# A 12-layer attention stack on one core: the scores of a tile issued as one block, and the value products cut to 64 rows by 64 columns

## The chip, the core and the metric

The kernel runs on one core of a Trainium2 chip. The time is device microseconds of one execution, lower is better; several runs are made and the median counts. TensorE (PE in the profile, with its weight loads shown apart as PEld), VectorE (DVE), ScalarE (ACT), GpSimd (POOL) and SyncE (SP, which issues the DMAs) each run a queue of their own in order, and wait for each other on semaphores.

## What is computed

The input is 2048 tokens of 128 channels. A stack of six layers runs on it, then a state space block (the "mamba" part), then the same six layers again. Half of each stack's output is added to its input. Each layer is attention in windows of 32 tokens, then a gated feed-forward part of 341 hidden units. Of the attention this is what matters here:

```python
def local_attention(q, k, v):            # 16 heads of 64, windows of w = 32
    nw = n // w
    bk2, bv2 = (look(bk), look(bv))      # a window and the one before it: 64 keys
    sim = jnp.einsum('bhwie,bhwje->bhwij', bq, bk2) * QK_SCALE
    sim = jnp.where(mask, -jnp.finfo(sim.dtype).max, sim)
    attn = jax.nn.softmax(sim, -1)
    out = jnp.einsum('bhwij,bhwje->bhwie', attn, bv2)
    return out.reshape(b, h, n, d)
...
out = local_attention(q, k, v).transpose(0, 2, 1, 3).reshape(b, n, INNER)
return out @ Wo
```

## The kernel before

**Tiles and steps.** The tokens are cut into 16 tiles of 128 (four windows each), so that a stack has 6 x 16 = 96 tiles and both stacks have 192. A tile passes through some six software-pipelined steps: at step s TensorE works on the k projection of tile s-19, the q projection of tile s-18, the value products of tile s-22 and so on. The loop over `s` in `tensor_stack` (L694 to L714) writes the order out by hand, and the other engines have loops of the same kind. Nothing else decides the order. Every fourth tile closes a chunk of 512 tokens, for which the feed-forward part runs. So four steps in a row differ: two are plain; one also has the centring product (L451) and the variance product (L471) of a chunk, one on each side of the P transposes, and its up products (L492 to L494) follow two blocks after the value products; one has the carry product (L341) and the down products (L550) between the scores and the P transposes. They are called the variance step and the down step below.

**PSUM.** It is used as four slots of two banks. Slot 0 takes the q and the k projection in turn. Slot 2 takes, in turn, the v projection, P transposed, and q transposed. Slot 3 takes the scores and the result of the value products. Slot 1 takes k transposed and small results. A block of TensorE waits until the last user's result has been read out.

**Scores.** For each of 8 head pairs, 4 windows and 2 heads of the pair one product is made: 32 queries by 64 channels against 64 channels by 64 keys (L349). It uses 64 rows and 32 columns of the array, so the array is cut in 8 parts that are used in turn; the two heads of a pair write to different banks. Eight mask products (L359) go ahead. The 64 products stand in two blocks: `scores_low` has head pairs 0 to 3, near the end of a step, and `scores_high` has 4 to 7, first in the next step. Between them stand the P transposes (L282) of the tile before. A float32 product is recorded as two pairs of weight load and matmul, so each half is "x64" in the trace.

**P and the value products.** `exponentials` (ScalarE, L996) writes P, GpSimd scales it by the reciprocal sums (L1774), and `p_transpose` turns it with 8 transposes, each with two heads' 64 keys stacked on 128 partitions. `p_evacuate` (L1010) copies the result from slot 2 to PTS, one activation for the upper 64 partitions and one for the lower. They go to different columns of PTS, which is 2048 wide and was set to zero at first (L1788 and, for the second stack, L1803). Each block of 64 columns is so block diagonal, and one product of 128 rows by 64 columns against 64 columns of PTS makes a window's output for both heads (`value_products`, L408): 32 of them for a tile, "x64" in the trace. `o_evacuate` (L1019) copies the result to OTS, and `out_products` (L428) multiplies by Wo. The values stand in V2, which ten small DMAs on SyncE's queue fill for each tile (`spread_values`).

**The chain of the rotation.** After the q projection ScalarE squares it (L921), and VectorE makes the two halves of the rotation from PSUM (L1304, L1313). Then slot 0 is free, and only then may the k projection begin. For k these are L934, L1322 and L1331, after which comes the next q projection. VectorE's order in a step is L1304, L1313, L1345 (sums of squares), [L1471 and L1473 after a down product], L1363 (row maximum of the scores), [L1403 and L1405 in a variance step], L1371 (scores minus maximum), L1322, L1389 and L1390 (residual), L1331, L1351, L1378 (row sums of P), L1382, L1357. The value products wait for L1371 of the next tile, since they write over its scores in slot 3.

Of the kernel before, what the change touches and what calls it, by code (L numbers as in the profile page):

```python
# [9 lines left out]
ACT = mybir.ActivationFunctionType  # L10
# [6 lines left out]
N = NT * NL  # L17
# [14 lines left out]
def build(nc, xT, consts, wqkv, wo, w1, w2, lpar, qks, mpar, in_w, xp_w, dt_w, out_w, out):  # L32
    ctx = ExitStack()
    with ctx:
# [3 lines left out]
        def sem(name):  # L38
            return ctx.enter_context(nc.semaphore("s_" + name))
# [23 lines left out]
        PS = ctx.enter_context(nc.psum_tensor("PS", [128, 4, 1024], F32))  # L63
        PSB = PS[:, :, :].rearrange("p s (h n) -> p (s h) n", h=2)
        top = [0]

        def take(n):
            top[0] += n
            assert top[0] <= 34400, top[0]
            return ARENA[:, top[0] - n:top[0]]  # L70

        def heads(ap, n=H):
            return ap.rearrange("p (h d) -> p h d", h=n)
# [19 lines left out]
        T2 = take(1024)  # L93
        KT = [take(1280) for _ in range(2)]
        SB, P, OTS = (take(1024) for _ in range(3))
        PTS = take(2048)
        V2 = [take(2048) for _ in range(2)]
        HG = take(1536)
        SX, RS, XC = HG[:, 0:512], HG[:, 512:1024], HG[:, 1024:1536]
# [34 lines left out]
        def unit(u):  # L134
# [10 lines left out]
        wo_in = [sem(f"wo_in{i}") for i in range(2)]  # L145
        w1_in, inw_in, mw_in = sem("w1_in"), sem("inw_in"), sem("mw_in")
        v2_in = [sem(f"v2_in{i}") for i in range(2)]
        eps_set, pad_set, zero_set, masks_set, edge_set, tab_set = (sem(n) for n in (
            "eps_set", "pad_set", "zero_set", "masks_set", "edge_set", "tab_set"))
        i_mu, i_sq, i_var, i_ln, i_rs, i_done = (sem("i_" + n) for n in (  # L150
            "mu", "sq", "var", "ln", "rs", "done"))
        x_hi, x_lo, w1_hi, w1_lo = (sem(n) for n in ("x_hi", "x_lo", "w1_hi", "w1_lo"))
# [7 lines left out]
        qT_ev, kT_ev, PT_ev, oT_ev = (sem(n + "_ev") for n in ("qT", "kT", "PT", "oT"))  # L160
# [37 lines left out]
        def tensor_stack(pe, r):  # L198
# [162 lines left out]
                            MK[a:b, 64:128].unsqueeze(1).broadcast_to([64, 8, 64]), start=True, stop=False,  # L361
                            skip_group_check=True)

            def scores_low(n):
                if not 0 <= n < N:
                    return
                pe.wait_ge(qT_ev, n0 + n + 1)
                pe.wait_ge(kT_ev, n0 + n + 1)
                pe.wait_ge(car_ev, n0 + n + 1)
                if n == 0:  # L370
                    pe.wait_ge(i_done, 4 * r + 4)
                    if r == 0:
                        pe.wait_ge(masks_set, 1)
                s = n + 20
                if (s - 24) % 4 == 3:
                    after_chunk(pe, f_h[1], (s - 24) // 4)
                after_tile(pe, oT_ev, s - 22)
                if s < RAMP or s >= N:
                    after_chunk(pe, f_h[1], (s - 23) // 4 - 1)
                    after_tile(pe, sub_done, s - 21)  # L380
                score_masks(n)
                score_tiles(n, range(4))

            def scores_high(n):
                if 0 <= n < N:
                    score_tiles(n, range(4, 8)).then_inc(S_done, 1)

            def p_transpose(n):
                if not 0 <= n < N:
# [8 lines left out]
                transposes(2, P, PT_done)  # L398

            def value_products(n):  # L400
                pt = PTS.rearrange("p (h w x) -> p h w x", h=8, w=4)
                v2 = V2[n % 2].rearrange("p (w h d) -> p w h d", w=4, h=8)
                for m in range(4):
                    for win in range(4):
                        for side in range(2):
                            hp, col = 2 * m + side, 32 * win
                            out = PS[64 * side:64 * side + 64, 3, 256 * m:256 * m + 256]
                            last = nc.tensor.matmul(  # L408
                                out.rearrange("p (a q) -> p a q", a=2)[:, :, col:col + 32], v2[:, win, hp, :],
                                pt[:, hp, win, :], start=True, stop=True, skip_group_check=True)  # L410
                last.then_inc(pv_done, 1)

            def values(n):
# [11 lines left out]
            def out_products(n, bank):  # L425
                w = WO[n // NT % 2]
                for j in range(8):
                    last = nc.tensor.matmul(PSB[:, bank, 0:128], w[:, 128 * j:128 * j + 128], OTS[:, 128 * j:128 * j + 128],  # L428
                                            start=j == 0, stop=j == 7)
                last.then_inc(wo_done, 1)  # L430

# [142 lines left out]
            def finish_tiles():  # L574
# [4 lines left out]
                    pe.wait_ge(sem, c0 + u + 1)  # L579

                u = UNITS - 3
                scores_high(94)
                tile(k_nrm, 95)
                tile(k_rot, 95)
                transposes(0, KN[1], kT_done)
# [108 lines left out]
            for s in range(115):  # L694
                if s == 19 + 1:
                    var_in(pe, r, 3)
                scores_high(s - 21)
                k_project(s - 19)
                out_project(s - 23)
                q_transpose(s - 20)  # L700
                values(s - 22)
                k_transpose(s - 20)
                ffn_up0(s - 24)
                ffn_up1(s - 24)
                ffn_up2(s - 24)
                q_project(s - 18)
                v_project(s - 20)
                scores_low(s - 20)
                carry(s - 19)
                ffn_centre(s - 23)  # L710
                ffn_down(s - 24)
                p_transpose(s - 21)
                ffn_variance(s - 23)
# [140 lines left out]
        def scalar_stack(act, r):  # L854
# [144 lines left out]
            def p_evacuate(n, slot=2):  # L999
                if not 0 <= n < N:  # L1000
                    return
                act.wait_ge(PT_done, n0 + n + 1)
                if n >= 1:
                    act.wait_ge(pv_done, n0 + n)
                else:
                    act.wait_ge(zero_set, r + 1)
                blocks = PTS.rearrange("p (b a q) -> p b a q", a=2, q=32)
                for par in range(2):
                    a, b = 64 * par, 64 * par + 64
                    last = act.activation(blocks[a:b, :, par, :], PS[a:b, slot, :].rearrange("p (b q) -> p b q", q=32), ACT.Copy)  # L1010
                last.then_inc(PT_ev, 1)

            def o_evacuate(n):
                if not 0 <= n < N:
# [698 lines left out]
        def pool_stack(pool, r):  # L1713
# [71 lines left out]
            if r == 0:  # L1785
                nc.gpsimd.memset(VT[1], 0.0)
                nc.gpsimd.memset(KT[1], 0.0).then_inc(pad_set, 1)
                nc.gpsimd.memset(PTS, 0.0).then_inc(zero_set, 1)  # L1788
            low_weights(0, 0)
            low_input(0)  # L1790
            low_weights(0, 1)
# [5 lines left out]
            for s in range(113):  # L1797
                if s == 17 + 1:
                    low_weights(0, 2)
                    low_input(1)  # L1800
                if s == 17 + 3 and r == 1:
                    pool.wait_ge(m_out, 4)
                    nc.gpsimd.memset(PTS, 0.0).then_inc(zero_set, 1)  # L1803
                if s == 17 + 5:
                    low_input(2)
                if s == 17 + 8:
                    low_input(3)
                ffn_low(s - 23)
                k_add_halves(s - 18)
                p_normalise(s - 20)  # L1810
                w_low_k(s - 18)
                q_normalise(s - 18)
                q_add_halves(s - 17)
                k_normalise(s - 18)
                input_low(s - 24)
                w_low_v(s - 19)
                w_low_q(s - 17)
# [259 lines left out]
```

## Time and profile before

| | |
|---|---|
| median of 3 runs | 3331.24 us (3329.32 to 3331.4) |
| span of the profiled execution | 3329.5 us |
| PE busy, and its weight loads | 3179.2 us (95%), 2524.1 us (76%) |
| DVE, ACT, POOL busy | 2793.2 us (84%), 2503.3 us (75%), 2435.9 us (73%) |
| TensorE share of the chain that ended last | 79% |
| value products L408, busy | 403.7 us |
| scores L349, busy | 326.0 us |
| copies of P transposed L1010, busy | 390.5 us |

A row of the timeline gives the start and the length of a merged run of instructions. A matmul is pipelined, and its recorded length holds some 0.2 us in which the next ones already run. So the time that a block takes on the engine is read from its start to the start of the next block, and not from its busy time. The "idle before" of a row is counted from the modelled end of the instruction before.

### The profile page before, as it was taken

How to read it: one execution, taken by the hardware profiler on the slowest of the kernel's cores; microseconds unless marked ns; L12 is line 12 of the kernel's file. 1: busy time of each engine (PE TensorE's matmuls, PEld its weight loads, DVE VectorE, ACT ScalarE, POOL GpSimd, SP SyncE). 2: the span in 40 equal slices, each digit the busy share in tenths (PEclk: the TensorE clock that was granted, in tenths of full speed). 3: DMA queues.
4: the chain of work that ended last, by engine and by line, in shares of the span. 5: the costliest groups of instructions: out<-in, count | busy, mean ns of one | idle time of the engine just before them, and what ended most of it. 6: DMA issues, size and time to landing. Idle time of an engine off the chain costs nothing.

```text
span 3329.5 us, 120453 instructions
## 1 busy us (share of the span) xinstructions
PE 3179.2 (95%) x51630; PEld 2524.1 (76%) x51630; DVE 2793.2 (84%) x3207; ACT 2503.3 (75%) x3160; POOL 2435.9 (73%) x1229
## 2 busy tenths in 40 slices
PE   7999999999999999998888999999999999999999
PEld 5888888888887887875333778788788888788777
DVE  7888888888888888877999888888888888888886
ACT  5777777777777777777676777777777777778776
POOL 6777777777777776672999768768768768768664
PEclk8999999999999999999999999999999999999999
DMA  3333333233233232221000323323323323323222
GB/s 120 84 75 87 74 82 89 71 86 88 67 90 85 67 90 65 65 72 38 30 0 0 97 67 81 86 69 86 89 70 82 95 67 80 96 65 85 69 65 69
DMA packets 142299, 245.22 MB, mean 74 GB/s; under 512 B 32397, under 2 KB 34638, under 8 KB 141774
## 3 DMA queue, kind: packets, MB, share of 16 engines
q1 hardware_dynamic: 141774, 237.51, 28.0%
q8 instruction: 415, 6.80, 0.9%
q14 instruction: 110, 0.90, 0.1%
HBM read 35.01 MB, written 1.05 MB: 11 GB/s over the span
## 4 chain that ended last, share of the span: by engine, by line
PE 79%; DVE 7%; issue 7%; POOL 4%; ACT 3%; DMA 0%; SPq 0%; DVEq 0%; POOLq 0%; ACTq 0%
PE PS L282 15%; PE PS L408 11%; PE PS L428 8%; PE PS L214 8%; PE PS L216 7%; PE PS L215 7%; PE PS L349 6%; PE PS L550 4%; ACT ARENA L955 3%; PE PS L492 2%; PE PS L494 2%; PE PS L493 2%; POOL ARENA L1868 2%; PE PS L451 2%; DVE ARENA L1681 2%
## 5 line engine op out<-in xcount | busy, mean ns | idle before, releaser
L1760 POOL TENSOR_TENSOR ARENA<-ARENA,RN 128x1024 f32<-128x1024 f32 x192 | 365.6, 1904 | 456.0 <-ACT RN L945 456.0
L282 PE MATMUL PS<-C,ARENA 128*128 128x128 f32 x4608 | 615.0, 277 | 42.9 <-ACT ARENA L955 16.4
L1752 POOL TENSOR_TENSOR ARENA<-ARENA 128x1024 f32<-128x1024 f32 x192 | 468.3, 2439 | 228.9 <-DVE ARENA L1331 228.1
L282 PEld LDWEIGHTS PS<-C,ARENA 128*128 128x128 f32 x4608 | 512.9, 141 | 119.7 <-issue 76.4
L214 PE MATMUL PS<-WL,XH 128*128 128x512 f32 x1152 | 489.7, 425 | 7.3 <-POOL XL L1719 4.0
L1010 ACT ACTIVATE ARENA<-PS 64x1024 f32<-64x1024 f32 x384 | 390.5, 1017 | 98.0 <-PE PS L282 94.6
L1746 POOL TENSOR_TENSOR ARENA<-ARENA 128x1024 f32<-128x1024 f32 x192 | 457.3, 2382 | 7.0 <-DVE ARENA L1313 7.0
L216 PE MATMUL PS<-WH,XH 128*128 128x512 f32 x1152 | 454.2, 394 | 0.0
L215 PE MATMUL PS<-WH,XL 128*128 128x512 f32 x1152 | 452.1, 392 | 0.0
L408 PE MATMUL PS<-ARENA 128*64 128x64 f32 x12288 | 403.7, 224 | 42.0 <-DVE ARENA L1371 26.0
L408 PEld LDWEIGHTS PS<-ARENA 128*64 128x64 f32 x12288 | 378.7, 139 | 77.1 <-issue 77.1
L1304 DVE TENSOR_TENSOR ARENA<-PS,TAB 128x1024 f32<-128x1024 f32 x192 | 235.0, 1224 | 230.5 <-ACT ARENA L921 230.5
L1774 POOL TENSOR_TENSOR ARENA<-ARENA,RI 128x1024 f32<-128x1024 f32 x192 | 365.9, 1906 | 47.2 <-DVE RI L1382 37.3
L428 PEld LDWEIGHTS PS<-ARENA 128*128 128x128 f32 x3072 | 372.2, 191 | 17.8 <-ACT ARENA L1019 1.5
L1768 POOL TENSOR_TENSOR ARENA<-ARENA,RN 128x1024 f32<-128x1024 f32 x192 | 374.2, 1949 | 1.5 <-ACT RN L945 1.5
L428 PE MATMUL PS<-ARENA 128*128 128x128 f32 x3072 | 373.7, 275 | 1.1 <-ACT ARENA L1019 1.1
L349 PEld LDWEIGHTS PS<-ARENA 64*32 64x32 f32 x24576 | 292.4, 105 | 69.3 <-issue 59.0
L349 PE MATMUL PS<-ARENA 64*32 64x64 f32 x24576 | 326.0, 223 | 0.1
L1363 DVE TENSOR_REDUCE MX<-PS 128x16 f32<-128x1024 f32 x192 | 234.2, 1220 | 94.8 <-PE PS L349 92.9
L1019 ACT ACTIVATE ARENA<-PS 128x1024 f32<-128x1024 f32 x192 | 197.1, 1027 | 139.0 <-PE PS L408 139.0
L921 ACT ACTIVATE ARENA<-PS 128x1024 f32<-128x1024 f32 x192 | 197.2, 1027 | 93.6 <-PE PS L216 93.6
L214 PEld LDWEIGHTS PS<-WL,XH 128*128 128x128 f32 x1152 | 218.3, 189 | 62.4 <-POOL XL L1719 4.8
(160 smaller groups left out, 6476.1 us busy)
## 6 DMA issues: line engine op xcount, KB each, us to landing
ARENA<-ARENA SPq DMA_DIRECT2D x1152, 128.0 KB
ARENA<-ARENA SPq DMA_DIRECT2D x768, 64.0 KB
ARENA<-in_wqkv SPq DMA_DIRECT2D x36, 512.0 KB, 5.1
ARENA<-in_wo SPq DMA_DIRECT2D x12, 512.0 KB, 3.9
ARENA<-in_w SPq DMA_DIRECT2D x12, 341.0 KB, 3.5
ARENA<-in_w SPq DMA_DIRECT2D x12, 192.0 KB, 3.9
X<-in_xT SPq DMA_DIRECT2D x4, 256.0 KB, 6.0
out<-X SPq DMA_DIRECT2D x1, 768.0 KB, 3.6
```

The costliest lines, as they stand in the source:

```text
L214: nc.tensor.matmul(o, XH[:, x], WL[:, s], start=True, stop=False)
L215: nc.tensor.matmul(o, XL[:, x], WH[:, s], start=False, stop=False)
L216: last = nc.tensor.matmul(o, XH[:, x], WH[:, s], start=False, stop=True)
L282: last = nc.tensor.transpose(PS[:, slot, 128 * j:128 * j + 128], src[:, 128 * j:128 * j + 128], ident)
L349: last = nc.tensor.matmul(PS[32 * win:32 * win + 32, slot, c:c + 64], q[a:b, hp, 32 * win:32 * win + 32], kt[a:b, hp, 32 * win:32 * win + ...
L408: last = nc.tensor.matmul(out.rearrange("p (a q) -> p a q", a=2)[:, :, col:col + 32], v2[:, win, hp, :], pt[:, hp, win, :], start=True, st ...
L428: last = nc.tensor.matmul(PSB[:, bank, 0:128], w[:, 128 * j:128 * j + 128], OTS[:, 128 * j:128 * j + 128], start=j == 0, stop=j == 7)
L1010: last = act.activation(blocks[a:b, :, par, :], PS[a:b, slot, :].rearrange("p (b q) -> p b q", q=32), ACT.Copy)
L1746: nc.gpsimd.tensor_tensor(QN[n % 2], QN[n % 2], P if n == 1 else T2, ALU.add).then_inc(q_add, 1)
L1752: nc.gpsimd.tensor_tensor(KN[n % 2], KN[n % 2], T2, ALU.add).then_inc(k_add, 1)
L1768: nc.gpsimd.tensor_tensor(a, a, bc(RN[:, n % 2, 16:32], 64), ALU.mult).then_inc(k_nrm, 1)
L1774: nc.gpsimd.tensor_tensor(heads(P), heads(P), bc(RI[:, n % 2, :], 64), ALU.mult).then_inc(p_nrm, 1)
```

## The change

The two score blocks become one, `scores`, where `scores_low` stood; the P transposes of the tile before then follow all 64 score products. P transposed is copied from PSUM by one activation over 128 partitions, to a PTS that is 1024 wide and has no zeros; both memsets of PTS are gone, and the first copy of the second stack waits for `m_out` itself. 1024 columns behind it are left unused. The value products are 64 instead of 32: each takes one head alone, 64 rows (its keys) by 64 columns (its channels) against 32 columns (its queries). The two heads of a pair use the upper and the lower 64 rows and write to different banks; two pairs use the left and the right 64 columns. OTS then holds the heads in another order, and `out_products` takes the blocks of Wo in that order.

```diff
-        PTS = take(2048)
+        PTS = take(1024)
+        take(1024)
...
-            def scores_low(n):
+            def scores(n):
...
                 score_masks(n)
-                score_tiles(n, range(4))
-
-            def scores_high(n):
-                if 0 <= n < N:
-                    score_tiles(n, range(4, 8)).then_inc(S_done, 1)
+                score_tiles(n, range(8)).then_inc(S_done, 1)
...
-                pt = PTS.rearrange("p (h w x) -> p h w x", h=8, w=4)
+                pt = heads(PTS, 8)
...
                     for win in range(4):
-                        for side in range(2):
-                            hp, col = 2 * m + side, 32 * win
-                            out = PS[64 * side:64 * side + 64, 3, 256 * m:256 * m + 256]
-                            last = nc.tensor.matmul(
-                                out.rearrange("p (a q) -> p a q", a=2)[:, :, col:col + 32], v2[:, win, hp, :],
-                                pt[:, hp, win, :], start=True, stop=True, skip_group_check=True)
+                        for par in range(2):
+                            for side in range(2):
+                                hp, a, b, col = 2 * m + side, 64 * par, 64 * par + 64, 32 * win
+                                o = 512 * par + 128 * m + col
+                                last = nc.tensor.matmul(
+                                    PS[64 * side:64 * side + 64, 3, o:o + 32], v2[a:b, win, hp, :],
+                                    pt[a:b, hp, col:col + 32], start=True, stop=True, skip_group_check=True)
...
+                    i = 2 * (j % 4) + j // 4
+                    last = nc.tensor.matmul(PSB[:, bank, 0:128], w[:, 128 * i:128 * i + 128], OTS[:, 128 * j:128 * j + 128],
...
-                scores_high(s - 21)
                 k_project(s - 19)
...
-                scores_low(s - 20)
+                scores(s - 20)
...
                 else:
-                    act.wait_ge(zero_set, r + 1)
-                blocks = PTS.rearrange("p (b a q) -> p b a q", a=2, q=32)
-                for par in range(2):
-                    a, b = 64 * par, 64 * par + 64
-                    last = act.activation(blocks[a:b, :, par, :], PS[a:b, slot, :].rearrange("p (b q) -> p b q", q=32), ACT.Copy)
-                last.then_inc(PT_ev, 1)
+                    act.wait_ge(m_out, 4 * r)
+                act.activation(PTS, PS[:, slot, :], ACT.Copy).then_inc(PT_ev, 1)
...
-                nc.gpsimd.memset(PTS, 0.0).then_inc(zero_set, 1)
...
-                if s == 17 + 3 and r == 1:
-                    pool.wait_ge(m_out, 4)
-                    nc.gpsimd.memset(PTS, 0.0).then_inc(zero_set, 1)
```

On TensorE, in a variance step, before (L359 masks, L349 scores, L451 centring product, L282 transposes of P, L471 variance product, L214 first product of the k projection):

```order
L359 MATMUL PS<-MK 32x512 x8
L349 MATMUL PS<-ARENA 32x64 x32
L451 MATMUL PS<-ARENA,C 128x512
L282 MATMUL PS<-C,ARENA 128x128 x8
L471 MATMUL PS<-ARENA,C 128x512
L349 MATMUL PS<-ARENA 32x64 x32
L214 MATMUL PS<-WL,XH 128x512
```

The same place after (the numbers of the lines are one higher or lower from here on: L350 scores, L450, L283 and L470 as L451, L282 and L471 before):

```order
L360 MATMUL PS<-MK 32x512 x8
L350 MATMUL PS<-ARENA 32x64 x64
L450 MATMUL PS<-ARENA,C 128x512
L283 MATMUL PS<-C,ARENA 128x128 x8
L470 MATMUL PS<-ARENA,C 128x512
L215 MATMUL PS<-WL,XH 128x512
```

The second block of 32 score products has moved ahead of the centring product, and the k projection now follows the variance product. In a plain step L451 and L471 are absent from both lists, and the transposes stood between the two score blocks.

On TensorE, later in a step, from the out products to the k transposes, before (L428 out products, L282 transposes of q and then of k, L408 value products):

```order
L428 MATMUL PS<-ARENA 128x128 x8
L282 MATMUL PS<-C,ARENA 128x128 x8
L408 MATMUL PS<-ARENA 64x2x32 x32
L282 MATMUL PS<-C,ARENA 128x128 x8
L492 MATMUL PS<-XNH,W1L 128x512
```

After:

```order
L427 MATMUL PS<-ARENA 128x128 x8
L283 MATMUL PS<-C,ARENA 128x128 x8
L406 MATMUL PS<-ARENA 64x32 x64
L283 MATMUL PS<-C,ARENA 128x128 x8
L491 MATMUL PS<-XNH,W1L 128x512
```

Nothing has moved here; 32 products over 64 columns (2 x 32) have become 64 over 32.

## Rows read from the trace of the kernel before

**Rows 1.** The page, its first part: busy us (share) x instructions.
```profile
PE 3179.2 (95%) x51630; PEld 2524.1 (76%) x51630; DVE 2793.2 (84%) x3207; ACT 2503.3 (75%) x3160; POOL 2435.9 (73%) x1229
```

**Rows 2.** Who waited for whom: engine line <- line: us in total, times, longest.
```profile
PE PS L408 <- DVE ARENA L1371: 26.0, 46, 1.3
...
PE PS L282 <- ACT ARENA L955: 16.4, 84, 0.2
```

**Rows 3.** A plain step, timeline, TensorE: start, length, line, [idle before].
```profile
1037.98 0.41 PE L359 MATMUL PS<-MK 64*32 64x512 bf16 x8
...
1038.21 0.84 PE L349 MATMUL PS<-ARENA 64*32 64x64 f32 x64
...
1039.26 1.06 PE L282 MATMUL PS<-C,ARENA 128*128 128x128 f32 x8 [0.21 <-ACT ARENA L955]
...
1040.25 0.86 PE L349 MATMUL PS<-ARENA 64*32 64x64 f32 x64
...
1041.04 0.50 PE L214 MATMUL PS<-WL,XH 128*128 128x512 f32 x1
...
1045.29 2.08 PE L408 MATMUL PS<-ARENA 128*64 128x64 f32 x64
...
1047.30 1.09 PE L282 MATMUL PS<-C,ARENA 128*128 128x128 f32 x8
...
1048.15 0.47 PE L214 MATMUL PS<-WL,XH 128*128 128x512 f32 x1
```

**Rows 4.** The scores of the first tile, timeline, TensorE: the same columns.
```profile
45.61 1.46 PE L349 MATMUL PS<-ARENA 64*32 64x64 f32 x128
47.78 0.47 PE L214 MATMUL PS<-WL,XH 128*128 128x512 f32 x1 [0.71 <-DVE ARENA L1313]
```

**Rows 5.** The same plain step, timeline, VectorE.
```profile
1038.91 1.21 DVE L1313 TENSOR_TENSOR ARENA<-PS,TAB 128x1024 f32<-128x1024 f32 x1
...
1045.55 1.22 DVE L1331 TENSOR_TENSOR ARENA<-PS,TAB 128x1024 f32<-128x1024 f32 x1
```

**Rows 6.** The rotation ahead of the second row of rows 4, VectorE.
```profile
46.31 1.21 DVE L1313 TENSOR_TENSOR ARENA<-PS,TAB 128x1024 f32<-128x1024 f32 x1
```

**Rows 7.** A down step, timeline, TensorE.
```profile
1009.20 0.84 PE L349 MATMUL PS<-ARENA 64*32 64x64 f32 x64
1009.97 0.70 PE L341 MATMUL PS<-ARENA,C 128*128 128x256 f32 x2
...
1013.09 1.04 PE L282 MATMUL PS<-C,ARENA 128*128 128x128 f32 x8
...
1014.84 0.50 PE L214 MATMUL PS<-WL,XH 128*128 128x512 f32 x1
```

**Rows 8.** A variance step, timeline, TensorE.
```profile
1051.31 0.84 PE L349 MATMUL PS<-ARENA 64*32 64x64 f32 x64
1052.09 1.12 PE L451 MATMUL PS<-ARENA,C 128*128 128x512 f32 x2
...
1055.75 0.50 PE L214 MATMUL PS<-WL,XH 128*128 128x512 f32 x1
```

**Rows 9.** The end of that variance step: TensorE's value products, and VectorE.
```profile
1060.51 2.08 PE L408 MATMUL PS<-ARENA 128*64 128x64 f32 x64 [0.45 <-DVE ARENA L1371]
...
1059.15 1.21 DVE L1371 TENSOR_TENSOR ARENA<-PS,MX 128x1024 f32<-128x1024 f32 x1
```

**Rows 10.** Durations in ns, min/median/max: L408 in one step, L349 and L428 everywhere.
```profile
L408 PE MATMUL PS<-ARENA x64: 222/222/270, 1019.1 to 1020.9; 128*64 128x64 f32 x64
...
L349 PE MATMUL PS<-ARENA x24576: 212/216/241, 45.6 to 3293.0; 64*32 64x64 f32 x200
...
L428 PE MATMUL PS<-ARENA x3072: 270/275/377, 76.2 to 3315.1; 128*128 128x128 f32 x192
```

**Rows 11.** What is under way on TensorE at 1027.38, in a score block begun at 1027.14.
```profile
1027.14 0.45 PE L349 MATMUL PS<-ARENA 64*32 64x64 f32 x31
```

**Rows 12.** The second stack's memset of PTS, timeline, GpSimd.
```profile
1841.61 1.80 POOL L1803 MEMSET ARENA<- 128x2048 f32 x1
```

More of the change, by code:

```diff
@@ L147, in build @@
         v2_in = [sem(f"v2_in{i}") for i in range(2)]
-        eps_set, pad_set, zero_set, masks_set, edge_set, tab_set = (sem(n) for n in (
-            "eps_set", "pad_set", "zero_set", "masks_set", "edge_set", "tab_set"))
+        eps_set, pad_set, masks_set, edge_set, tab_set = (sem(n) for n in (
+            "eps_set", "pad_set", "masks_set", "edge_set", "tab_set"))
         i_mu, i_sq, i_var, i_ln, i_rs, i_done = (sem("i_" + n) for n in (
@@ L427, in out_products @@
                 for j in range(8):
-                    last = nc.tensor.matmul(PSB[:, bank, 0:128], w[:, 128 * j:128 * j + 128], OTS[:, 128 * j:128 * j + 128],
+                    i = 2 * (j % 4) + j // 4
+                    last = nc.tensor.matmul(PSB[:, bank, 0:128], w[:, 128 * i:128 * i + 128], OTS[:, 128 * j:128 * j + 128],
                                             start=j == 0, stop=j == 7)
@@ L581, in finish_tiles @@
                 u = UNITS - 3
-                scores_high(94)
                 tile(k_nrm, 95)
```

## The prediction

> **What bounds the kernel now.** I began with the busy shares: PE 95%, the next engine 84% [rows 1]. A busy share of pipelined matmuls proves little, so the next view is who waited for whom. The waits of TensorE are short: in the stacks the largest two are 26 us in 46 places for VectorE's L1371, and 16.4 us in 84 places for ScalarE's L955 [rows 2]. All else is TensorE going from one block to the next. So a change is worth what it takes from TensorE's own sequence, until another chain becomes the later one. The third view is therefore the timeline of each kind of step, read from a block's start to the next block's start.
>
> **One score block, plain step.** Before, from the masks (1037.98) to the k projection (1041.04) there are 3.06 us [rows 3]. In it the first 64 scores take 1.05 to the start of the transposes; in the down step the same block takes 0.77 to its successor (1009.20 to 1009.97) [rows 7]. The 0.28 between is the wait for L955, which reads the v projection out of slot 2 before the transposes may write there.
>
> The new sequence is made of pieces that the trace shows. Masks to scores is 0.23 [rows 3]. The first tile already has all scores in one block, since no transposes are due there: recorded length 1.46 [rows 4], against 0.84 for half. A half gives its place to the successor 0.07 before its recorded end (0.84 against 0.77), so the whole takes 1.39. Transposes with a projection behind them take 0.85 (1047.30 to 1048.15), while those with scores behind them take 0.99 (1039.26 to 1040.25) [rows 3]. Sum: 0.23 + 1.39 + 0.85 = 2.47, and the transposes now come 0.23 + 1.39 = 1.62 after the masks instead of 1.28, so the wait for L955 is gone. The gain is 3.06 - 2.47 = 0.59, of which 0.28 is the wait and 0.31 the switches between kinds of block.
>
> What is late next? The k projection needs slot 0, so it waits for L1313, which ends at 1038.91 + 1.21 = 1040.12 [rows 5]. Where TensorE is known to have waited for it, it began 0.26 after its end (47.78 against 46.31 + 1.21 = 47.52) [rows 4, 6]. That is 1040.38 here; TensorE would arrive at 1037.98 + 2.47 = 1040.45. The gain just fits, with 0.07 to spare; this chain starts at the q projection, ahead of everything that the change touches.
>
> **Down step.** From L349 to the k projection 5.64 (1009.20 to 1014.84), with 3.12 for L341 and L550 (1009.97 to 1013.09) [rows 7]. After: 1.39 + 3.12 + 0.85 = 5.36, so 0.28 less.
>
> **Variance step.** From 1051.31 to 1055.75 there are 4.44 [rows 8]. The first block's 0.77 becomes 1.39, the second (0.79, as 1040.25 to 1041.04 [rows 3]) goes, and some 0.1 of switching with it: about 0.27 less. But the value products of this step already wait for L1371, 0.45 us of idle time, and start at 1060.51 where L1371 ends at 60.36 [rows 9]. Ahead of L1371 VectorE has L1403, which needs the chain from the variance product, and that product is issued 0.6 later than before. So I count 0.06 here.
>
> **Sum of the scores.** The 192 tiles are 48 groups of four steps: 2 x 0.59 + 0.28 + 0.06 = 1.52 us, times 48 = 73 us. The bounds are the switches alone, without any recovered wait (2 x 0.31 + 0.28 = 0.9, so 43 us), and with the variance step at its full 0.27 (83 us). The score semaphore comes earlier too, which nobody on the path waits for: VectorE takes the maximum in its own order behind L1345.
>
> **Value products.** Nothing in this trace runs 64 by 64 parts, so I work out the pace from both sides. The 64 matmuls have a length of 2.08 us together [rows 3], one of them 0.22 [rows 10], so they start (2.08 - 0.22) / 63 = 29.5 ns apart, and with two parts of the array in turn a part has one every 59 ns. The product is not longer than the load: 64 columns more add 275 - 222 = 53 ns. The load of 64 columns, seen bare on the first two products, costs 270 - 222 = 48 ns [rows 10]. So load and product of a part overlap, and a load that starts as the product before it starts sets the pace of 59 ns by itself, with some ns for the handing over. The change halves what is streamed (27 ns) but not the load's 64 columns. With four parts at once, 128 / 4 x 59 ns = 1.89 us; today 64 / 2 x 59 ns = 1.89 us. I take no change. The lower bound is the pace at which score products come, (1.46 - 0.22) / 127 = 9.8 ns [rows 4], so 1.25 us for 128: 0.6 less. The upper bound is a load and a product in turn, 59 + 27 = 86 ns, so 2.75 us: 0.86 more. Zero lies where it does because the score block, which is cut by rows as well, does overlap: its load of 32 columns costs 241 - 216 = 25 ns and its product 53 [rows 10]; in turn that is 78 ns for eight parts, 9.8 each, and only some 24 could have begun 0.24 us into a block, where the trace has 31 [rows 11].
>
> There is a rule against this change. The Trainium skill, TensorE: Matmul & The Clock Gate (Part 3, The mechanism), says that a weight load runs under products in flight only where the row group differs. Left and right parts share their rows, so by it the block before would take 64 x (48 + 53) ns = 6.5 us; it takes 2.01 (1045.29 to 1047.30 [rows 3]), so this trace contradicts it. By the rule the new block would have 64 x (48 + 27) ns = 4.8 us in each half, and the kernel would end some 530 us later; the sum above doesn't use it.
>
> **The copy and the zeros.** ScalarE saves a copy of 1.02 us a tile. It was hidden: the q transposes that need slot 2 come two blocks later, and ScalarE then waits for the k projection anyway. In the drain of each stack the copies stand nearer to the path; I count 1 us there for both. GpSimd's memset in the second stack (1.80 [rows 12]) stands ahead of a k addition while the pipeline fills: 0 to 1.8 us, I take 1. PTS without zeros and the order of Wo cost nothing.
>
> **The sum.** 73 + 1 + 1 = 75 us from the span of 3329.5. The median of the runs is 1.7 above that span, so 3331.2 - 75 = 3256.
>
> **Rivals.**
>
> *The waits come back.* TensorE meets the rotation with 0.07 to spare. If the k projection waits for L1313 by what it saved, a plain step keeps 0.31: 3256 + 48 x 2 x 0.28 = 3283. For it: the small margin. Against: the chain has fixed lengths in every plain step.
>
> *Faster value products.* If the pace is that of issue, 0.6 less a tile. Of that a plain step can use: the q projection, moved to 1048.15 - 0.59 = 1047.56, may start no earlier than 45.55 + 1.22 + 0.26 = 47.03 [rows 5], so 0.53. Four steps give about 2.1, times 48 = 101 us: 3155. The overlap at 59 ns with a load of the same size speaks against it. The Trainium skill, TensorEngine Tiling (Array Packing), Theoretical Speedup, promises up to twice the speed per dimension of at most 64, which would be this case.
>
> *Slower value products, and a slower kernel.* Load and product of a part take turns when the array is cut both ways at 64: 0.86 more a tile, all on the path, 165 us: 3421. It outweighs the scores from 75 / 192 = 0.39 us a tile on, which is a part's round of 71 ns instead of 59. Against it stand the 31 products of rows 11, though those are parts of 32 columns.
>
> **How the numbers follow.** Forecast 68%, with its own range 3235 to 3280 (bounds of the scores, plus a few ns a round). Waits come back 10%, faster products 10%, slower ones 12%. Forecast and first rival together give 78%; 3215 to 3290 holds them and a partial gain in the products. A measurement of this kernel tells about 0.2% from no change. Faster by more than that 87%, within it 2%, slower 11%.
>
> **What would show it.** Right: score blocks of 128 of 1.4 to 1.5 us in all tiles; the wait of the P transposes for L955 gone; masks to k projection near 2.47 in plain steps; value products 2.0 us from start to start. Wrong: that block at 1.3 or 2.7; a wait of the k projection for the rotation of more than 0.1; a variance step that has grown.

## The result, and the profile after

The changed kernel takes 3429.93 us in the median of 4 runs (3428.65 to 3438.7), the kernel before 3330.93 (4 runs). The ratio is 1.030, with an interval of 1.0287 to 1.0316: 99 us slower, where 75 us faster was forecast. The profiled execution of after has a span of 3427.4 us.

**What was changed works as planned.** A plain step of after, timeline, TensorE (start, length, line, count; L360 masks, L350 scores, L283 transposes, L215 first product of a projection, L406 value products; L1364 on VectorE is the subtraction that was L1371):

```profile
1056.09 0.41 PE L360 MATMUL PS<-MK 64*32 64x512 bf16 x8
1056.32 1.46 PE L350 MATMUL PS<-ARENA 64*32 64x64 f32 x128
1057.71 1.09 PE L283 MATMUL PS<-C,ARENA 128*128 128x128 f32 x8
1058.56 0.47 PE L215 MATMUL PS<-WL,XH 128*128 128x512 f32 x1
...
1062.77 2.07 PE L406 MATMUL PS<-ARENA 64*64 64x32 f32 x128
1064.77 1.09 PE L283 MATMUL PS<-C,ARENA 128*128 128x128 f32 x8
```

From the masks to the k projection there are 2.47 us, where there were 3.06 [rows 3], and no row has a wait. The value block takes 2.00 from start to start, where it took 2.01 [rows 3].

**Where the time went.** Three groups of the page of after (busy, mean ns | idle before, and what ended most of it), and three rows of its waits (in total, times, longest):

```profile
L406 PE MATMUL PS<-ARENA 64*64 64x32 f32 x24576 | 407.5, 221 | 100.4 <-issue 60.6
...
L350 PE MATMUL PS<-ARENA 64*32 64x64 f32 x24576 | 296.8, 225 | 40.6 <-issue 40.3
...
L1004 ACT ACTIVATE ARENA<-PS 128x1024 f32<-128x1024 f32 x192 | 196.3, 1022 | 188.5 <-PE PS L283 188.5
```

```profile
PE PS L406 <- issue: 60.6, 32, 4.5
PE PS L350 <- issue: 40.3, 62, 1.7
PE PS L406 <- DVE ARENA L1364: 39.7, 42, 1.7
```

Busy time has hardly grown: 407.5 us for the value products against 403.7, and the copy of P transposed went from 390.5 to 196.3. What is new is idle time *inside* the two dense blocks that ends with "issue", that is with nothing that the profile shows as awaited. One such place, timeline of TensorE, in the middle of the value products of a tile, and the up products (L491 to L493) behind it:

```profile
322.09 1.95 PE L406 MATMUL PS<-ARENA 64*64 64x32 f32 x118 [0.82 <-DVE ARENA L1364]
328.21 0.53 PE L406 MATMUL PS<-ARENA 64*64 64x32 f32 x10 [4.18 <-issue]
328.67 1.97 PE L283 MATMUL PS<-C,ARENA 128*128 128x128 f32 x8
...
331.29 0.63 PE L493 MATMUL PS<-XNH,W1H 128*128 128x512 f32 x1
331.72 0.63 PE L491 MATMUL PS<-XNH,W1L 128*128 128x512 f32 x1
...
334.65 0.40 PE L492 MATMUL PS<-XNL,W1H 128*128 128x512 f32 x1
334.88 0.40 PE L493 MATMUL PS<-XNH,W1H 128*128 128x512 f32 x1
```

After 118 of the block's 128 recorded products (two for each of the 64) TensorE stands still for over 4 us, though nothing between the products of a block is awaited. Then comes a second loss: the big products start 0.43 us apart (331.29 to 331.72), and from 334.65 on 0.23 apart. The windows view tells why (length, busy and count of PE, PEld, DVE, ACT and POOL, granted clock, DMA share, GB/s): the clock of TensorE is at half, 1.2 instead of 2.4 GHz, for 6.8 us.

```profile
324.00:327.00 3.00, 0.03 (x2) 0.00 (x0) 3.00 (x3) 0.00 (x0) 2.09 (x1) 1.00 0.83 333
327.70:334.50 6.80, 6.29 (x28) 5.34 (x28) 0.54 (x1) 4.02 (x4) 1.65 (x1) 0.50 0.00 0
```

**What TensorE waits for is its own instructions.** One DMA queue has grown. Its row on the page (packets, MB, share of the DMA engines), before and then after:

```profile
q8 instruction: 415, 6.80, 0.9%
```

```profile
q8 instruction: 511, 8.37, 1.1%
```

That is 16 KB a packet in both, and the packets come all through the execution: the program's instructions are fetched while it runs. After has 130,997 records of TensorE (products, weight loads, and semaphore instructions), which is 256 to a packet; the change adds 2 x 64 of them a tile (32 products more, each recorded as two pairs of load and matmul), 192 x 128 / 256 = 96 packets. I numbered TensorE's records in order and set the packets beside them. In after there are 123 places where TensorE stands still and goes on 1.2 to 1.6 us (median 1.38) after a packet of q8 has landed. In 118 of the 123 the first record after the stop is number 449 counted from the first record that the packet before held, so 64 short of the end of what it has. No view shows which packet holds which record: the borders are counted in steps of 256 from the start of the trace. What the trace does show is that these places lie a multiple of 256 records apart, and that packets and such places go together one by one. The reverse is the stronger evidence: in all eleven traces, those of the experiments below among them, the record at such a place never starts earlier than 1.1 us after its packet has landed, whether TensorE stops there or not, while in after the record just ahead of it starts up to 3.4 us before the landing. In the example no packet starts from 318.5 to 325.8, and one starts here (DMA view of 325.8 to 326.0):

```profile
q1 hardware_dynamic: 19, 0.07, 89.7%
q8 instruction: 1, 0.02, 29.8%
```

It took 0.95 us, so it landed at about 326.85, and TensorE went on at 328.21, 1.36 later. The packet began 5.9 us after TensorE had reached the 193rd record of the packet before; the median in after is 1 us.

I call this a stop, and count for each kernel the stops, their time, and the time at half clock. The last can be worked out from the mean clock: 2 x (1 - 0.979) x 3427.4 = 144 us for after and 2 x (1 - 0.993) x 3329.5 = 47 for before; the trace's own record of the clock, used in the table, has 149 and 49.

| | median us | packets | stops | us in stops | us at half clock |
|---|---|---|---|---|---|
| before | 3330.9 | 415 | 1 | 0.3 | 49 |
| after | 3429.9 | 511 | 123 | 128.0 | 149 |
| scores in one block alone | 3294.6 | 415 | 54 | 34.6 | 52 |
| value products and copy alone | 3398.0 | 511 | 38 | 46.1 | 104 |
| scores in one block, borders moved | 3275.2 | 416 | 26 | 11.4 | 42 |
| the same, moved elsewhere | 3302.4 | 416 | 56 | 40.1 | 48 |
| after, borders moved by 52 | 3515.8 | 512 | 148 | 184.4 | 246 |
| after, borders moved by 184 | 3493.0 | 512 | 140 | 159.7 | 207 |

A microsecond at half clock costs about half of itself. That is an estimate, since idle time at half clock costs nothing. For after it makes 128 + (149 - 49) / 2 = 178 us of loss. If the merge of the scores is worth some 70 us (shown below), 3331 - 70 + 178 = 3439, and 3430 was measured. The same sum gives 3544 and 3500 for the last two rows, so it comes out 7 to 28 us too high.

**Which steps pay.** From one step's masks to the next, mean over both stacks: a plain step takes 13.13 us in before and 13.18 in after (its median went from 13.11 to 13.05), a down step 16.45 and 16.26, and a step with variance and up products 19.49 and 21.64. The last alone gives 44 x 2.15 = 95 of the 99 us. The plain steps pay as well, though their mean hides it: 68 of the stops, 59 us, lie in them and use up what the merge gains there; 46, with 74 us, lie in the variance steps.

### The profile page after: what moved, and what is told of

Same layout as the page of the kernel before. It is cut to its first block, busy times and chain, and to the rows that moved or that the text cites. A ratio compares the mean times of both kernels' runs of the same rounds, so it can differ in the third digit from the quotient of the medians.

```text
span 3427.4 us, 144835 instructions
## 1 busy us (share of the span) xinstructions
PE 3171.4 (93%) x63918; PEld 2553.8 (75%) x63918; DVE 2782.4 (81%) x3207; ACT 2309.0 (67%) x2968; POOL 2428.7 (71%) x1227
## 3 DMA queue, kind: packets, MB, share of 16 engines
q1 hardware_dynamic: 141774, 237.51, 27.2%
HBM read 35.01 MB, written 1.05 MB: 11 GB/s over the span
## 4 chain that ended last, share of the span: by engine, by line
PE 80%; issue 8%; DVE 7%; POOL 3%; ACT 2%; DMA 0%; SPq 0%; DVEq 0%; POOLq 0%; ACTq 0%
PE PS L283 15%; PE PS L406 11%; PE PS L427 8%; PE PS L350 7%; PE PS L215 7%; PE PS L217 7%; PE PS L216 7%; PE PS L549 4%; PE PS L491 2%; PE PS L492 2%; PE PS L493 2%; PE PS L360 2%; DVE ARENA L1674 2%; PE PS L450 1%; DVE ARENA L1364 1%
## 5 line engine op out<-in xcount | busy, mean ns | idle before, releaser
L283 PE MATMUL PS<-C,ARENA 128*128 128x128 f32 x4608 | 634.4, 281 | 51.1 <-issue 29.7
L283 PEld LDWEIGHTS PS<-C,ARENA 128*128 128x128 f32 x4608 | 525.7, 143 | 125.6 <-issue 88.0
L215 PE MATMUL PS<-WL,XH 128*128 128x512 f32 x1152 | 502.0, 436 | 6.6 <-POOL XL L1712 3.3
L406 PE MATMUL PS<-ARENA 64*64 64x32 f32 x24576 | 407.5, 221 | 100.4 <-issue 60.6
L406 PEld LDWEIGHTS PS<-ARENA 64*64 64x64 f32 x24576 | 384.9, 136 | 136.4 <-issue 136.4
L350 PE MATMUL PS<-ARENA 64*32 64x64 f32 x24576 | 296.8, 225 | 40.6 <-issue 40.3
L350 PEld LDWEIGHTS PS<-ARENA 64*32 64x32 f32 x24576 | 283.2, 105 | 61.7 <-issue 51.0
L1012 ACT ACTIVATE ARENA<-PS 128x1024 f32<-128x1024 f32 x192 | 197.0, 1026 | 188.7 <-PE PS L406 188.7
L1004 ACT ACTIVATE ARENA<-PS 128x1024 f32<-128x1024 f32 x192 | 196.3, 1022 | 188.5 <-PE PS L283 188.5
L993 ACT ACTIVATE ARENA<-ARENA 128x1024 f32<-128x1024 f32 x192 | 202.7, 1056 | 107.9 <-DVE ARENA L1364 103.9
L918 ACT ACTIVATE ARENA<-PS 128x1024 f32<-128x1024 f32 x192 | 197.2, 1027 | 99.5 <-PE PS L217 99.5
L215 PEld LDWEIGHTS PS<-WL,XH 128*128 128x128 f32 x1152 | 220.8, 192 | 56.3 <-issue 15.8
## 6 DMA issues: line engine op xcount, KB each, us to landing
ARENA<-ARENA SPq DMA_DIRECT2D x1152, 128.0 KB, 2.4
```

Of the source, the lines that this page charges most:

```text
L215: nc.tensor.matmul(o, XH[:, x], WL[:, s], start=True, stop=False)
L283: last = nc.tensor.transpose(PS[:, slot, 128 * j:128 * j + 128], src[:, 128 * j:128 * j + 128], ident)
L350: last = nc.tensor.matmul(PS[32 * win:32 * win + 32, slot, c:c + 64], q[a:b, hp, 32 * win:32 * win + 32], kt[a:b, hp, 32 * win:32 * win + ...
L406: last = nc.tensor.matmul(PS[64 * side:64 * side + 64, 3, o:o + 32], v2[a:b, win, hp, :], pt[a:b, hp, col:col + 32], start=True, stop=True ...
```

## The experiments

**The two halves of the change, each alone.** The first kernel is before with `scores_low` and `scores_high` merged; the second is after with the score block cut in two again, at the places of before.

```diff
-                scores_high(s - 21)
                 k_project(s - 19)
...
-                scores_low(s - 20)
+                scores(s - 20)
```

> The kernel before with one edit: all 64 score products in one block; value products (32 of 128 rows), two-part copy and memsets as before. In the changed kernel TensorE stops 109 times, 123 us in all, inside blocks of scores and value products, each time until about 1.3 us after a 16 KB packet of its instruction queue (q8) has landed; the kernel before has next to none of this. Theory A (instructions arrive too late where 256 of them are used up in less than about 3.3 us): here the number of packets stays at 415 and only the masks-and-scores run of 272 instructions is dense, so a few stops remain, about 15 of 1.3 us; 3255 to 3285 us. Theory B (the merged score block itself is what costs, by waits on slots 0 and 2 that came back): slower than before, 3340 or more, with waits of the k projection on L1313 or of the transposes on L955. Theory C (the 64-row value products cost, for whatever reason): 3256, no stops.

> The changed kernel with the scores in two blocks again: only the value products, the one-pass copy and the missing memsets are new. The number of q8 packets is 511 as in the changed kernel. Theory A: the value block of 256 instructions in 1.85 us and the three score runs are dense; about 20 to 60 stops of 1 to 2 us, plus half clock behind some of them; 3360 to 3420 us. Theory B (merged block costs): 3331, as before, since the value block takes 1.85 us from first to last start as it did. Theory C: 3430 + 75 = 3505, the merge's gain of 75 us being lost again and the rest staying.

The merge alone: 3294.57 us, ratio 0.989 (0.9879 to 0.9908). Theory A had forecast 15 stops and 3255 to 3285 us: there are 54, so it was right in kind and too low in amount. The value products alone: 3398.03, ratio 1.020 (1.0185 to 1.0219), inside theory A's range and far from what the other two gave. So one half gains 35 us and the other loses 67; together they would be 32 slower, but are 99 slower: the halves harm each other. Both have stops (table). A plain step and the value block (L404) of the merge, timeline, TensorE, and its group of scores (L349) in the list of lines:

```profile
1027.37 1.33 PE L349 MATMUL PS<-ARENA 64*32 64x64 f32 x112
1029.60 0.35 PE L349 MATMUL PS<-ARENA 64*32 64x64 f32 x16 [0.91 <-issue]
1029.88 1.09 PE L282 MATMUL PS<-C,ARENA 128*128 128x128 f32 x8
...
1034.94 2.08 PE L404 MATMUL PS<-ARENA 128*64 128x64 f32 x64
1036.96 1.09 PE L282 MATMUL PS<-C,ARENA 128*128 128x128 f32 x8
```

```profile
L349 PE MATMUL PS<-ARENA 64*32 64x64 f32 x24576 | 292.5, 225 | 23.8 <-issue 23.7
```

The merge adds no instruction, yet it stops TensorE 54 times: the 64 score products are 128 recorded pairs of load and product, so 256 records, a whole packet, and they take 1.24 us from first to last start. Before, the same 256 had the transposes of P and more in between. Of all stretches of 256 records in a row (stops taken out), 4.5% are shorter than 3.3 us in before, 10.9% in the merge, 11.3% in the second kernel and 16.2% in after. 3.3 us is what the packet needs where it comes in time: it begins 0.84 after TensorE's record 193 (the median in before), takes 1.05 and is used 1.38 after that (the medians in after). For the second kernel, lines again (L410 value products, L350 scores):

```profile
L410 PE MATMUL PS<-ARENA 64*64 64x32 f32 x24576 | 403.2, 220 | 60.9 <-issue 36.4 <-DVE ARENA L1370 24.2
...
L350 PE MATMUL PS<-ARENA 64*32 64x64 f32 x24576 | 326.8, 223 | 2.3 <-issue 2.3
```

Its stops lie in the value products and in the transposes behind them, and with 46 us of stops and (104 - 49) / 2 = 27 of half clock it would be at 3404; 3398 was measured.

**Is it the other DMA traffic that makes packets late?** The packets share the DMA engines with SyncE's queue (q1), and in the example the engines were 83% busy just while the packet was awaited. So the copies into V2 were cut, first to 16 of 512 columns a row (in after and in before), then to one row a copy with all its columns (in after). From the third tile on these kernels leave the filling of V2 out, so their value products work on incomplete data.

```diff
-                    sp.dma_start(v2[a:a + 32, 0, :], last[:, c]).then_inc(v2_in[n % 2], 16)
+                    sp.dma_start(v2[a:a + 32, 0, 0:e], last[:, c]).then_inc(v2_in[n % 2], 16)
```

> The changed kernel with the ten DMAs a tile into V2 cut to 16 columns instead of 512 from tile 2 of each stack on (the value products then read old values: part of the data movement is left out). Nearly all of the 237 MB of traffic goes. Theory A1 (packets of instructions come late because they queue behind this traffic): the long delays from 2 to 12 us between the need and the start of a packet go, most stops go, 3260 to 3310 us. Theory A2 (the delay is the fetch path's own, about 1 us to start, 1 us to land and 1.3 us to be used): stops stay, 3390 to 3430 us.

> The control for the run before: the kernel before with the same thin DMAs (same part left out). It has almost no stops, so both theories expect 3320 to 3331 us; a larger gain would mean that the DMAs cost something else too, which then has to be taken off the other run's gain.

> The changed kernel with the ten DMAs a tile into V2 cut to one row each from tile 2 of each stack on (old values are read; part of the data movement is left out). The thin DMAs of the earlier run had as many packets as before; here nearly all of the 142000 packets go. If packets of instructions start late because other packets stand before them, the starts that came 3 to 6 us late go, and stops fall from 128 us to under 70: 3330 to 3370 us. If the lateness is the fetch path's own: 3415 to 3430 us.

Measured: 3422.85 (ratio 1.028, 1.0258 to 1.03), 3331.49 (1.000, 0.9994 to 1.0014) and 3421.42 (1.027, 1.0233 to 1.0306). The DMA view of the third of these kernels, and its value products in the list of lines:

```profile
DMA packets 76217, 53.49 MB, mean 16 GB/s; under 512 B 62477, under 2 KB 64718, under 8 KB 75598
...
q1 hardware_dynamic: 75598, 44.23, 4.7%
q8 instruction: 511, 8.37, 1.0%
```

```profile
L406 PE MATMUL PS<-ARENA 64*64 64x32 f32 x24576 | 407.3, 221 | 88.9 <-issue 55.4 <-DVE ARENA L1364 33.3
```

With 19% of q1's bytes and 53% of its packets (more than the forecast thought would stay) there are still 117 stops with 120.6 us, instead of 123 with 128.0. In the first of the three q1 keeps the DMA engines busy for 5.7% of the span instead of 27.2%, and there are as many stops as in after. So the traffic is not what makes most packets late. The 7 to 9 us by which the two kernels are faster than after can't be told from none: the two runs of the third took 3411 and 3432 us. The control shows that the copies cost nothing where there are no stops.

**Does the place of the packets' borders in the program matter?** If TensorE runs dry because 256 dense instructions follow a border, then moving all borders, with nothing else changed, must change the time. Small products of no use (16 columns, 4 records each) ahead of the first stack, and ahead of the second, do that: four steps of the merge have some 2175 records, which is close to 8.5 packets, so the borders come back to nearly the same places in the loop again and again.

```diff
             if r == 0:
                 pe.wait_ge(const0_in, 16)
+                for _ in range(12):
+                    nc.tensor.matmul(PSB[0:32, 7, 0:16], ident[:, 0:32], onesd[:, 0:16], start=True, stop=True)
...
             pe.wait_ge(f_done, UNITS)
+            for _ in range(4):
+                nc.tensor.matmul(PSB[0:32, 6, 0:16], ident[:, 0:32], onesd[:, 0:16], start=True, stop=True)
```

> The merged scores alone (the kernel of run e1_scores, 3294.6 us, 54 stops of 34.6 us in all) with 12 small products more on TensorE ahead of the first stack and 4 ahead of the second: 48 and 16 instructions, under 1 us of work. All the stops of the runs so far stand at one place of TensorE's instruction count: 449 after a multiple of 256 (64 before the end of a second packet of 256), and four steps take 2175 instructions, so that two such groups are 17 packets less 2 and the packets' borders stay at nearly the same places of the program all along. Theory A (a packet that comes too late): the added instructions move the borders from the ends of the score block to its middle; from the time in which 256 instructions are used up at each border I reckon a third of the stops or less, 5 to 15 us; 3262 to 3276 us. Rival (the stops belong to the place in the program, as a bank or a semaphore would make them): 3294 to 3296, stops as before.

> The same with 26 small products (104 instructions) ahead of the first stack and none ahead of the second: the borders move to the worst place, where a window of 256 instructions holds the whole score block. Theory A: nearly twice the stops of the run without products, 50 to 70 us; 3310 to 3335 us. Rival: 3295.

Measured: 3275.16 (ratio 0.983, 0.9815 to 0.9848) and 3302.4 (0.991, 0.9892 to 0.9932). Sixteen useless products make the merge 19 us *faster*, and 26 make it 8 us slower (that step is small: the intervals of the two ratios overlap a little). But for these products the program is the same in all three, so a bank or a semaphore at some place in it doesn't explain the 19 us; the place of the borders does. The scores in the first of them, list of lines, and a step of it, timeline:

```profile
L349 PE MATMUL PS<-ARENA 64*32 64x64 f32 x24576 | 284.4, 224 | 5.8 <-issue 5.2
```

```profile
1029.20 0.41 PE L359 MATMUL PS<-MK 64*32 64x512 bf16 x8
1029.43 1.46 PE L349 MATMUL PS<-ARENA 64*32 64x64 f32 x128
1030.82 1.13 PE L447 MATMUL PS<-ARENA,C 128*128 128x512 f32 x2
...
1037.23 1.06 PE L282 MATMUL PS<-C,ARENA 128*128 128x128 f32 x8 [0.30 <-ACT ARENA L1006]
1038.64 2.08 PE L404 MATMUL PS<-ARENA 128*64 128x64 f32 x64 [0.35 <-DVE ARENA L1367]
```

The idle time of the scores fell from 23.8 to 5.8 us. The second kernel was forecast at 3310 to 3335 us and came out better.

**The same for the whole change.** Here the reckoning failed. 13 and 5 small products, and then 46 and 6, were put where the trace of after had most room behind the borders.

> The changed kernel (3429.9 us, 123 stops of 128 us, 149 us at half clock) with 13 and 5 small products ahead of the stacks (52 and 20 instructions). Its value block is dense too, so no place of the borders is free of stops. Theory A: the windows reckon to about half of the stops, 50 to 75 us, and less half clock; 3335 to 3370 us. Rival: 3430.

> The changed kernel whole, with 46 small products of no use (184 instructions) ahead of the first stack and 6 more (24) ahead of the second, so that the borders of the 256-instruction packets lie 184 and 208 instructions earlier in the program, where the trace of the changed kernel has no dense block behind a packet that was asked for late. Theory A (TensorE runs out of instructions where a packet begins late, so that the place of the borders decides; a packet is asked for only when the sequencer is past the last wait before the border): the stops fall from 128 us to 60 to 90 us, and with the half clock that follows them the time is 3355 to 3400 us. Theory B (what e7 showed is that any shift only costs, or the loss is one of amount and not of place): 3430 us or more, with 120 us of stops or more.

Measured: 3515.8 (ratio 1.055, 1.0536 to 1.0567) and 3492.96 (1.050, 1.0476 to 1.0526): both far slower than after, where both were forecast faster. The value products of the two, lists of lines:

```profile
L406 PE MATMUL PS<-ARENA 64*64 64x32 f32 x24576 | 427.8, 222 | 177.8 <-issue 139.9 <-DVE ARENA L1366 37.9
```

```profile
L406 PE MATMUL PS<-ARENA 64*64 64x32 f32 x24576 | 424.1, 221 | 147.3 <-issue 114.4 <-DVE ARENA L1366 32.9
```

So 18 useless products cost 86 us. The stops lie where they did in the count of records, though that is another place of the program: the gaps of over 0.2 us ahead of that one record in each 256 add up to 146 us in after, 194 in the first of these kernels and 168 in the second, and ahead of no other record of the 256 to more than 15. That confirms that the borders decide where TensorE stops, and shows that I can't yet say from a trace which place is good. Two things were read from the traces, and not tested. First, in all these kernels the packet behind a stop begins late: in after 119 packets that follow a stop began 2.29 us after record 193 in the median, the other 388 after 0.84; in the kernel with 13 and 5 it is 2.42 and 0.93. So late packets follow stops more often; which is cause and which effect was not tested. Second, packets begin late where TensorE waits for a semaphore a few instructions ahead of the border, as at the start of the value products behind L1364: in the two kernels above, packets whose record 192 lies in the out products and whose border lies in the value products began 2.3 us after record 193 in the median. The second of these already stood in the forecast for the kernel with 46 and 6, which had 60 to 90 us of stops where 159.7 came. What sets the moment at which a packet is asked for stays open.

## Why the prediction was wrong

**The step that failed** is the cost of issuing the two dense blocks, in "Value products" and in "One score block, plain step". The first priced the 64 products on the array alone ("With four parts at once ... I take no change") and bounded them by two paces of the array; the second took the 1.39 us of the merged scores from a first tile and let it hold for all. That the change adds 24,576 instructions, and that the merged score block puts 256 of them into 1.24 us, was costed at nothing, without naming the condition for it: that the instructions are there in time. Measured one by one, the merge gives 35 us where 73 were forecast, and the value products with copy and zeros lose 67 where 2 were to be gained. What the sum lacks is 128 us of stops and some 50 us from the clock behind them, 178 in all, where forecast and result are 174 apart. The page of before had the row for it, 415 instruction packets of 16 KB; divided by the instructions it tells that 256 score products' records must last as long as a packet takes to come. What that is couldn't be read there: before has one stop.

**The terms of the sum**, by its own steps:
- *Plain step.* 3.06 to 2.47 was forecast, and 2.47 is what the rows show. The wait for L955 is gone. The margin of 0.07 us to the rotation held: in all of after the projections waited for it (L1306 there) once, for 0.7 us.
- *All kinds of step.* Read in the merge with moved borders, where stops weigh least, from masks to masks in the median: plain 13.11 to 12.47 (forecast 0.59, measured 0.63), down 15.90 to 15.66 (0.28, 0.24), variance 19.37 to 19.40 (0.06, -0.03). 48 x (2 x 0.63 + 0.24 - 0.03) = 71 us, against 73. The doubt about the variance step was right: the value products wait for VectorE there, 39.7 us in 42 places in after against 26.0 in 46 [rows 2]. The "about 0.27 less" ahead of its k projection was mis-sized, though: from masks to k projection this step went from 4.66 to 3.99 us in the median, 0.67 less. What the sum overlooked is the gap behind the variance product, 1.04 us when scores follow it (two rows of the timeline of before, below) and 0.54 when the k projection does. All of it was given back in after: the k projection took 1.79 instead of 1.49, for a reason that no row gives, and the wait for VectorE took the rest (q transposes to value products 1.49 to 1.85). So the 0.06 came out near because VectorE's chain sets this step, as the prediction said, and not by the size of what TensorE saves.

```profile
1053.92 1.11 PE L471 MATMUL PS<-ARENA,C 128*128 128x512 f32 x2
1054.96 0.86 PE L349 MATMUL PS<-ARENA 64*32 64x64 f32 x64
```

- *Value block.* 2.00 against 2.01 from start to start, so "no change" was right as to the array, and its first and last products start 1.85 us apart (1.86 before). The Trainium skill, TensorEngine Tiling (Array Packing), Theoretical Speedup, has up to 2x for a dimension of at most 64; here rows halved and the streamed columns halved give 1.00x. That the 59 ns of a load and its handing over set the pace fits, but no run tested it.
- *The copy.* It was called hidden, and nearly is. With the new order and the two old copies the q transposes wait for the second one (0.30 in the row of L282 above, 11.4 us in 36 places in that kernel), and in after they never wait for the copy. But that wait lies in the variance step, ahead of the one for VectorE: from the out products to the value products the step takes 3.67 us in the kernel with moved borders and 3.63 in after, in the median, so I estimate 44 x 0.04, about 2 us.

**The rivals.** "Slower value products" gave 3421, near the 3430 measured, but for a reason that didn't happen: the round of a part would have grown from 59 to 71 ns or more, and the block from 1.89 towards 2.75; it stayed at 1.85. The waits didn't come back, and the products didn't get faster. The true cause was no rival, so the range, made of the cases named, couldn't hold it.

**The best version** is the merge of the scores without the new value products, with 12 and 4 small products ahead of the stacks: 3275.16 us, 1.7% faster than before and 4.5% faster than after. Its last 19 us hang on where the borders fall, so they have to be measured anew after every edit that changes the number of instructions.

## What to carry to other kernels

On an engine that issues thousands of small instructions, count them as a load of their own: find the queue of the instruction packets on the page, divide, and compare the time of the densest stretch of one packet's instructions with what a packet needs from its start to its use. A change that packs more and smaller instructions closer together pays there, even when each costs the array nothing. Idle time before an instruction inside a block, released by nothing ("issue"), is a sign of it. To test it, compare the place of each such stop in the count of instructions, modulo 256, with the landing of the packets, and put a few useless instructions ahead of the loop.

## What the runs showed of the hardware

- TensorE's instructions come in packets of 16 KB, 256 at a time. Where they come late, TensorE stops 64 short of the end of the last packet it has (118 of 123 stops, the borders counted from the start of the trace), and goes on 1.2 to 1.6 us after the next has landed; in eleven traces never less than 1.1 us after it. The Trainium skill, TensorE: Matmul & The Clock Gate, gives TensorE a reorder window 64 deep; the 64 here agrees with it in size, which is no proof that it is the same.
- A packet takes 0.9 to 1.9 us. It begins 0.8 to 1.2 us after TensorE has reached the 193rd record of the packet before, in the medians of the kernels, but in after one in twenty begins over 5 us after it, and some begin 0.3 us ahead of it, so reaching that record can't be all that starts it. With a fifth of the other queue's bytes the medians in after went from 0.97 to 0.94 and 0.91 us.
- Behind stops, and elsewhere when TensorE was idle, its granted clock is at half for up to 10.2 us at a time (in after an idle time of 1.1 to 4.5 us came shortly before each); big products then start 0.43 us apart instead of 0.23. In after there are 100 us more at half clock than in before, so a stop costs more than its length.
- 128 tiled products (a load and a matmul each) start within 1.24 us in the merged score block, 9.8 ns apart, so that 256 instructions are used up long before the 3.3 us are over that a packet needs.
